# Delta rule on one core: where the 32x32 corners, lower blocks and joins are made and kept

## The reference, cut to what matters

```python
q, k, v = (silu(causal_conv4(h @ W)) for W in (Wq, Wk, Wv))
gk   = -exp(A_log) * softplus(h @ Wgk + dt_bias)
beta = sigmoid(h @ Wb + b_b)
q, k = l2norm(q) * DK ** -0.5, l2norm(k)
for t in range(128):                          # per sequence and head
    S = S * exp(gk[t])
    delta = (v[t] - k[t] @ S) * beta[t]
    S = S + outer(k[t], delta)
    o[t] = q[t] @ S
o = o * rsqrt(mean(o * o) + 1e-5) * g_norm * silu(h @ Wg)
return o.reshape(128, 1536) @ Wo
```

## Time and profile before

| what | value |
|---|---|
| median of 3 runs | 1293.94 us (1293.71 to 1302.33) |
| the profiled execution, own time | 1289.78 us |
| its span, first to last instruction | 1288.0 us |
| mean granted TensorE clock | 0.914 of full |
| busy share of the span | PE 85%, PEld 55%, DVE 60%, ACT 51%, POOL 26% |
| joins and corners, first group | 549.75 to 563.4 us |
| joins and corners, second group | 661.3 to 676.6 us |
| joins and corners, third group | 776.1 to 789.1 us |

### The profile page before, as it was taken

The page is one execution under the profiler, slowest core; times in us unless marked ns, Lnnn a source line. Parts: engine busy times, 40 slices in busy tenths (PEclk is TensorE's granted clock), DMA queues, the critical chain, the costliest instruction groups (busy, mean ns, idle before and its releaser), DMA issues. The chain is left out here.

```text
span 1288.0 us, 24654 instructions
## 1 busy us (share of the span) xinstructions
PE 1090.4 (85%) x9386; PEld 708.9 (55%) x9387; DVE 767.9 (60%) x2041; ACT 662.2 (51%) x1389; POOL 329.3 (26%) x337
## 2 busy tenths in 40 slices
PE   6998786788899877789869867987899988888998
PEld 3565554455656533367446636866344444576776
DVE  4566657686754487968886695566353465462211
ACT  2565354453532254886786563554766352354342
POOL 1333300134000046555465520230000045600000
PEclk9999997699999976979969985988999988899999
DMA  8000000200000000000000000080568510000000
GB/s 316 1 2 1 3 3 1 101 1 1 3 1 1 1 0 1 1 2 2 1 1 2 1 1 2 1 365 2 108 125 181 117 18 1 2 3 1 1 1 17
DMA packets 18324, 44.76 MB, mean 35 GB/s; under 512 B 4992, under 2 KB 8096, under 8 KB 17568
## 3 DMA queue, kind: packets, MB, share of 16 engines
q1 hardware_dynamic: 18208, 43.20, 11.7%
HBM read 42.41 MB, written 0.79 MB: 34 GB/s over the span
## 5 line engine op out<-in xcount | busy, mean ns | idle before, releaser
L223 POOL TENSOR_TENSOR norm_rstd<-norm_var,norm_power 128x4 f32<-128x4 f32 x24 | 24.6, 1025 | 309.6 <-DVE norm_var L216 309.6
L954 ACT ACTIVATE L_xattn_pT<-banks 128x512 f32<-128x512 f32 x128 | 69.0, 598 | 64.3 <-PE banks L829 64.3
L1022 DVE TENSOR_REDUCE L_xattn_top<-banks 128x4 f32<-128x512 f32 x128 | 79.5, 683 | 34.8 <-PE banks L798 34.5
L1668 DVE TENSOR_TENSOR L_ffn_a<-L_ffn_a,L_ffn_share 128x512 f32<-128x512 f32 x64 | 39.8, 685 | 60.1 <-DMA L_ffn_share<-L_ffn_shares 56.4
L1895 ACT ACTIVATE L_ffn_aT<-banks,L_ffn_shift 128x512 f32<-128x512 f32 x64 | 43.3, 687 | 58.9 <-PE banks L1847 57.3
L1582 PE MATMUL banks<-L_ffn_a,region_a 128*128 128x512 f32 x136 | 67.5, 601 | 5.2 <-DVE L_ffn_a L1668 5.2
L1908 DVE SCALAR_TENSOR_TENSOR x<-banks,L_ffn_combine,x 128x128 f32<-128x128 f32 x64 | 18.0, 344 | 88.5 <-PE banks L1858 88.5
L1573 PE MATMUL banks<-hT,region_a 128*128 128x512 f32 x136 | 68.3, 608 | 0.0
L1858 PEld LDWEIGHTS banks<-region_b,L_ffn_aT 128*128 128x128 f32 x512 | 59.4, 192 | 6.7 <-issue 6.7
L502 ACT ACTIVATE L_attn_p<-banks,L_attn_shift 128x129 f32<-128x129 f32 x128 | 45.4, 368 | 34.0 <-DVE L_attn_shift L555 34.0
L1737 PE MATMUL banks<-hT,region_a 128*128 128x512 f32 x128 | 59.6, 609 | 1.3 <-PEq L78 1.3
(11 more groups left out here) (557 smaller groups left out, 2888.6 us busy)
## 6 DMA issues: line engine op xcount, KB each, us to landing
L_ffn_share<-L_ffn_shares SPq DMA_DIRECT2D x32, 512.0 KB, 10.3
region_b<-in_L_ffn SPq DMA_DIRECT2D x1, 6216.0 KB, 29.7
region_a<-in_L_ffn SPq DMA_DIRECT2D x1, 4416.0 KB, 13.5
region_b<-in_L_attn SPq DMA_DIRECT2D x1, 3150.5 KB, 10.3
region_a<-in_L_ffn SPq DMA_DIRECT2D x1, 3080.5 KB, 16.4
region_b<-in_L_attn SPq DMA_DIRECT2D x1, 1633.5 KB, 9.4
region_b<-in_L_xattn SPq DMA_DIRECT2D x1, 835.0 KB, 7.7
w_tables<-in_tables SPq DMA_DIRECT2D x1, 832.0 KB, 11.7
```

Of the source, the lines that this page charges most:

```text
L954: nc.scalar.activation(pT[:, n % 2, 4 * i:4 * i + 4, :], rows_of(flip[i][:], 4), ACT.Exp, scale=scale).then_inc(exped, 1)
L1022: nc.vector.tensor_reduce(top[:, 32 * i + 24:32 * i + 28], rows_of(score[i][:], 4), X, ALU.max).then_inc(topped, 1)
L1668: nc.vector.tensor_tensor(a[:, k % AHEAD, :], a[:, k % AHEAD, :], share[:, batch % RING, j, :], ALU.mult).then_inc(weighed, 1)
```

## The change

- The lower corners are no longer made by matmuls. `keep_low` transposes on DVE the upper corner of block row 0 out of the PSUM bank into `half_inverse`. `place_upper(2)` now goes ahead of `keep_low(0)` and `place_upper(0)` between the two.
- The joins are kept in memory of their own (`c[:, 4]`, a value tile that is free then), all by ACT; the waits for `place_upper` go, and DVE's `keep_join` goes.
- `keep_lower` moves from ACT to POOL, between the third `add_taps` and the first `square_tile` of the next group, with drains around each copy.
- `keep_corners` copies block row 2 first, and block row 0 after a wait for `low_kept`.
- On ACT the first two taps of the next group's fourth tile move ahead of `keep_join`, the third ahead of `keep_corners`, and the fourth behind `keep_carry` of step 0 of the value loop.
- `project_values` has its two banks exchanged (6 and 5, before 5 and 6), with the waits that go with them.

```diff
-    joined = blocks[:].rearrange("p t s -> p (t s)").rearrange("p (b h s) -> p b h s", b=B, h=G)
+    joined = c[:, 4, :, :].rearrange("p b (h s) -> p b h s", h=G)
...
-    bank_gate, bank_half = bank[4:6], bank[5:7]
+    bank_gate, bank_half = bank[4:6], (bank[6], bank[5])
...
+            def keep_lower(hg):
+                pool.wait_ge(lower_ready, hg + 1)
+                after(pool, carry_made, B * hg)
+                for b in (0, 1):
+                    pool.drain()
+                    nc.gpsimd.tensor_copy(half_inverse[BLOCKS[b], :, :, BLOCKS[b]].rearrange("p b h s -> p (b h) s"),
+                                          lower_c[BLOCKS[b], :, :].rearrange("p s q -> p q s")).then_inc(lower_kept, 1)
+                pool.drain()
...
                     for m in range(3):
                         add_taps(first + B + m)
+                keep_lower(hg)
+                if more:
                     square_tile(first + B, sq)
                     add_taps(first + B + 3)
...
             def project_values(hg, H):
                 if H == 0:
+                    pe.wait_ge(lower_ready, hg)
+                elif H == 1:
                     pe.wait_ge(corner_kept, 2 * hg)
                     pe.wait_ge(low_kept, 2 * hg)
-                elif H == 1:
-                    pe.wait_ge(upper_ready, 4 * hg)
...
                 pe.wait_ge(join_kept, 2 * hg + half + 1)
-                pe.wait_ge(join_kept_too, 2 * hg + half + 1)
...
                 last.then_inc(corner_made, 1)
-                for i in range(16):
-                    n, h = 4 * half + i // G, i % G
-                    last = nc.tensor.matmul(bank_join[half][BLOCKS[1], NB * i:NB * i + NB], AT[BLOCKS[1], n, h, BLOCKS[1]],
-                                            joined[BLOCKS[1], n, h, :], start=True, stop=True)
-                last.then_inc(low_made, 1)
...
             def keep_join(hg, half):
                 act.wait_ge(join_made, 2 * hg + half + 1)
-                act.wait_ge(upper_ready, 4 * hg + 2)
-                nc.scalar.activation(joined[BLOCKS[3], 4 * half:4 * half + 4, :, :].rearrange("p b h s -> p (b h s)"),
-                                     bank_join[half][BLOCKS[3], :], ACT.Copy).then_inc(join_kept_too, 1)
...
+                for b in (1, 3):
+                    last = nc.scalar.activation(joined[BLOCKS[b], 4 * half:4 * half + 4, :, :].rearrange("p b h s -> p (b h) s"),
+                                                rows_of(bank_join[half][BLOCKS[b], :], 16), ACT.Copy)
+                last.then_inc(join_kept, 1)
...
-                for b in (0, 2):
+                for b in (2, 0):
+                    if b == 0:
+                        act.wait_ge(low_kept, 2 * hg + half + 1)
...
-                keep_lower(hg, 0)
-                keep_lower(hg, 1)
+                if more:
+                    scale_tap(first + B + 3, 0)
+                    scale_tap(first + B + 3, 1)
                 keep_join(hg, 0)
                 keep_join(hg, 1)
                 if more:
-                    scale_tap(first + B + 3, 0)
-                    scale_tap(first + B + 3, 1)
+                    scale_tap(first + B + 3, 2)
                 keep_corners(hg, 0)
-                if more:
-                    scale_tap(first + B + 3, 2)
-                    scale_tap(first + B + 3, 3)
                 keep_corners(hg, 1)
...
                         keep_carry(k)
+                    if more and s == 0:
+                        scale_tap(first + B + 3, 3)
                     if more and s < 2:
                         silu(first + B + 2 + s)
...
             def keep_low(hg, half):
-                dve.wait_ge(low_made, 2 * hg + half + 1)
+                dve.wait_ge(corner_made, 2 * hg + half + 1)
                 after(dve, carry_made, B * hg)
-                nc.vector.tensor_copy(half_inverse[BLOCKS[1], 4 * half:4 * half + 4, :, 0:NB].rearrange("p b h s -> p (b h) s"),
-                                      rows_of(bank_join[half][BLOCKS[1], :], 16)).then_inc(low_kept, 1)
+                nc.vector.transpose(half_inverse[BLOCKS[1], 4 * half:4 * half + 4, :, 0:NB].rearrange("p b h s -> p (b h) s"),
+                                    bank_join[half][BLOCKS[0], :]).then_inc(low_kept, 1)
...
                 place_upper(1)
                 place_upper(3)
-                keep_join(hg, 0)
-                keep_join(hg, 1)
                 place_upper(2)
+                keep_low(hg, 0)
                 place_upper(0)
-                keep_low(hg, 0)
                 keep_low(hg, 1)
```

More of the change, by code:

```diff
@@ L2937, in delta_rule @@
              "blocks_act", "blocks_taken", "rest_copied", "row_done", "product_made", "rest_done", "values_made", "r_ready", "lower_ready", "upper_ready",
-             "join_made", "join_kept", "join_kept_too", "lower_kept", "corner_made", "corner_kept", "low_made", "low_kept",
+             "join_made", "join_kept", "lower_kept", "corner_made", "corner_kept", "low_kept",
              "carry_made", "carry_kept", "far_made", "far_kept", "y_made", "z_kept", "o_made", "squares_ready",
@@ L2945, in delta_rule @@
      blocks_act, blocks_taken, rest_copied, row_done, product_made, rest_done, values_made, r_ready, lower_ready, upper_ready,
-     join_made, join_kept, join_kept_too, lower_kept, corner_made, corner_kept, low_made, low_kept,
+     join_made, join_kept, lower_kept, corner_made, corner_kept, low_kept,
      carry_made, carry_kept, far_made, far_kept, y_made, z_kept, o_made, squares_ready,
```

## The result

The changed kernel takes 1299.91 us (median of 20 runs, 1294.43 to 1306.68) against 1293.99 us before (20 runs, 1291.42 to 1302.33): ratio 1.0041, 95% interval 1.0027 to 1.0055, about 5 us slower by the ratio (the medians are 5.9 apart). The prediction was 1297, range 1290 to 1302, no change by its bound of 1%, with the forecast's sum at +3.5.

What follows compares the result with a forecast made beforehand. No engine alone bounds it; the first two groups' path runs ACT's last tap, POOL's additions and square, PE. Terms -2.5 + 2 x 1.5 + 2 x 1.5 = +3.5 us on 1293.94, rounded to 1297; range 1290 to 1302.

Steps and rivals of the forecast that it cites:

- Path through POOL: First two groups: path runs ACT's last tap, POOL's additions 6.6 us, POOL's square 1.9, PE; the carry not on it before.
- Third group: Lower blocks to step 1, with no next tiles: PE goes on at 788.3 against 790.81, 2.5 us gained.
- Later tap: First two groups: POOL copies of 2.5 us hold the carry, fourth tap behind it comes 1.5 us later a group.
- copies under 2.0 us: POOL's lower-block copies: below about 2.0 us each, ACT's corner copies end about as late and little depends on copy time.
- Clock: First two groups: PE idle 4.4 us, then half rate for 3.5 us, losing 1.5 us a group; bounds 0 and 3.
- The sum: Whole kernel: -2.5 for the third group, 2 x 1.5 for the tap, 2 x 1.5 for the clock, +3.5 us.
- the clock holds: Rival, chance 0.25: PE keeps its clock after the idle time, sum +0.5, 1294.5 us; 1292.5 with copies of 2.0 or less.
- the slow copies: Rival, chance 0.2: POOL's copies at the carry's wait slower than forecast; 1299.5 us at 3.0 each, 1304 at 4.0.
- nothing passes on: Rival, chance 0.05: third group's 2.5 us lost in step 1 to PE's lower clock, POOL's delay made up; about 1294.
- the fast rival: Rival, chance 0.1: additions not on the path, first two groups each gain the carry's lead of 1.9 us or more; 1285.6.

Runs made afterwards that it cites:

- experiment 2: Changed kernel with POOL's three additions of the fourth tile spread over steps 1, 2 and 3, that tile's silu in step 4: ratio 0.9925 to the kernel before.
- experiment 4: Kernel before the change, with only POOL's three additions of the fourth tile spread over steps 1, 2 and 3 and the silu moved: ratio 0.996 to it.
- experiment 7: Changed kernel with each of POOL's two copies of the lower blocks issued twice: ratio 1.0065 to the kernel before.
- experiment 1: Changed kernel with three extra 128x512 matmuls on PE in step 1 of the first two groups, into an unread bank: ratio 1.0001 to the kernel before.
- experiment 8: Changed kernel with the value halves' banks and waits as before the change: ratio 1.0022 to the kernel before.
- experiment 3: Changed kernel with ACT's fourth tap put back ahead of the corner copies, beside the third: ratio 0.9989 to the kernel before.

## Why the prediction came out as it did

- **Path through POOL:** right. PE and ACT both wait for the additions (4.79 and 4.02 us); experiments 2 and 4 show it by taking the additions away. In the kernel before the carry isn't on that path. In the changed one it is, as the prediction has it, because the fourth tap now stands behind it: experiment 7 moves the carry and the additions by the same 3.7 us.
- **Third group:** right, -2.5 forecast. PE went on 2.33 us sooner, and the group to the next stage was 2.65 shorter. The transpose out of PSUM took 0.71 where 0.70 was taken.
- **Later tap:** right in place, mis-sized. Each copy took 1.89 us, not 2.5; it sits at the price of POOL's straight square, although it reads one word in 32. So the carry led by 3.0 and 2.8 us, not 1.9, and the additions came 0.5 us later in each group (11.60 against 11.06, 13.30 against 12.70), not 1.5. As the prediction says of copies under 2.0 us, ACT's last corner copy (to 564.95) then ends as late as PE's carry (564.74). The estimate worked out from the Trainium skill, "GPSIMD Engine Reference", section 7, was 2.5 too; that section's table is about kernels written for POOL's Q7 cores, the trace does not agree with it for this copy, and its 1.89 decides.
- **Clock:** right in kind, mis-sized the other way: 2.8 and 2.5 us a group (experiment 1), not 1.5, though within the bound of 3. The term that was too small is how long the clock stays low. I took 3.5 us from the first gate's idle time; it was 6.7, from 574.4 to 581.1. The kernel before had that case too, behind the second gate's idle time of 4.12 us:

```profile
759.00:765.70 6.70, 5.66 (x7) 2.44 (x8) 6.70 (x35) 2.80 (x6) 0.00 (x0) 0.50 0.00 0
```

At the same share it would have given 3.0. PE's idle time was 4.79 and 3.38 us, where 4.4 was worked out for both groups: in the second, PE's work ahead of it took 7.8 us, not the 6.8 taken from before, because the clock was still at 0.50 from the carry (680.42) to 686.9.

- **The sum:** +3.5 against +3.26 for the stage, by two errors that cancel: 2 x 1.0 too much for the tap and about 2.3 too little for the clock. That the sum came so close is luck. The runs moved by more than the stage, 5.3 us by the ratio, and the prediction has no term for that rest; it isn't explained here either.
- **Rivals:** "the clock holds" is out (0.50 behind both idle times), and so are the slow copies (1.89 us each), "nothing passes on" (the third group kept its 2.65) and the fast rival. The fast rival has its place in another kernel: with the additions off the path (experiments 2 and 4) the lead of the carry is paid out in part.

## What to carry to other kernels

Work that is brought forward ahead of a wait which stays where it is becomes idle time of the engine, and on PE that idle time can cost more than the whole delay: here, in each of two groups, 0.5 us of lateness and about 2.7 us of lower clock. Before a stretch is shortened, find the queue that gates the step behind it; spreading three additions over POOL's later steps turned a ratio of 1.0041 into 0.9925. And where a sum of estimates is right, check its terms one by one before trusting them for the next case.

## What the runs showed of the hardware

- The length of PE's idle time alone did not say what the clock would cost. The loss was 2.7 and 2.5 us after 3.11 and 3.39 us (experiment 8), 1.5 after 3.84 and 4.02 (experiment 3), and nothing after 3.64 (experiment 7, second group) or after 2.2 (experiment 1). It went with the time at 0.50 that followed: 6.7 and 6.8 us in the changed kernel (losses 2.8 and 2.5), 3.3 in experiment 3 (1.5).
- PE's clock came back sooner with work that nobody reads: one 128x512 matmul of 2.07 us in the third group took 4.9 us off it against experiment 2, and 2.1 against the quickest third group without it (56.2, experiment 1).
- POOL copied 32x1024 words, read one in 32, in 1.89 us, where ACT needed 1.98 for the same copy; a DVE transpose of 32x512 out of PSUM took 0.71 us.
